# The order of transfers on SyncE in a two-layer graph network: the graph result first, an output's reads one slot later

## The reference: what is computed

```
x = layernorm(x + (adj @ x) @ W0 + b0)
h = x
for _ in range(3):
    a = adj @ h                            # a_in and a_out are the same here
    av = concat([a, a])
    z  = sigmoid(av @ w3.T + w3_b + h @ u3.T + u3_b)
    r  = sigmoid(av @ w4.T + w4_b + h @ u3.T + u3_b)
    hv = tanh(av @ w5.T + w5_b + (r * h) @ u5.T + u5_b)
    h  = (1 - z) * h + z * hv
out = layernorm(x + h)
```

## Time and profile before

| | |
|---|---|
| device time, median of 3 runs | 1645.3 us (1638.58, 1645.3, 1648.38) |
| the profiled execution: its own time | 1646.79 us |
| its span, first to last instruction | 1645.0 us |
| granted TensorE clock, mean | 0.99 |
| busy: PE, DVE, ACT, POOL | 1603.0, 1425.3, 945.5, 262.0 us |
| the DMA queue's packets | 50.4% of 16 engines' span |

### The profile page before, as it was taken

The page is one execution under the profiler, slowest core; times in us unless marked ns, Lnnn a source line. Parts: engine busy times, 40 slices in busy tenths (PEclk is TensorE's granted clock), DMA queues, the critical chain, the costliest instruction groups (busy, mean ns, idle before and its releaser), DMA issues.

```text
span 1645.0 us, 21680 instructions
## 1 busy us (share of the span) xinstructions
PE 1603.0 (97%) x7676; PEld 1350.1 (82%) x7676; DVE 1425.3 (87%) x1902; ACT 945.5 (57%) x1365; POOL 262.0 (16%) x296
## 2 busy tenths in 40 slices
PE   8899999999999999999999999999999999999994
PEld 8788888888888888888888888888888888888883
DVE  5788889898898898888989889899889898898886
ACT  3665555555565666555655556565556555655553
POOL 4011111122111121111211111112021121110002
PEclk9999999999999999999999999999999999999997
DMA  5343536555355653565535564455644555445543
GB/s 165 103 149 133 167 103 197 175 183 174 112 185 192 195 173 111 162 209 187 179 109 173 184 202 152 140 168 177 207 151 144 179 181 178 128 161 172 180 166 115
DMA packets 195132, 268.26 MB, mean 163 GB/s; under 512 B 18896, under 2 KB 166864, under 8 KB 195024
## 3 DMA queue, kind: packets, MB, share of 16 engines
q1 hardware_dynamic: 195024, 266.88, 50.4%
HBM read 134.68 MB, written 132.12 MB: 162 GB/s over the span
## 4 chain that ended last, share of the span: by engine, by line
PE 78%; DMA 10%; DVE 6%; SPq 4%; issue 1%; ACT 1%; POOL 0%; ACTq 0%; DVEq 0%; POOLq 0%
PE ps_r L316 38%; PE ps_h L316 25%; PE ps_a L376 6%; PE ps_l L342 5%; SPq L219 3%; PE ps_l L331 2%; DMA h_scratch_a<-h_blocks_a 2%; DMA h_scratch_b<-h_blocks_b 2%; DMA h_scratch<-h_blocks 2%; DMA a_landed<-a_scratch_a 2%; DVE a_blocks L696 1%; DMA a_landed<-a_scratch_b 1%; DVE hv L736 1%; DVE hv L733 1%; DMA x_in_b<-x 1%
## 5 line engine op out<-in xcount | busy, mean ns | idle before, releaser
L563 ACT ACTIVATE rh<-ps_r,bias_r 128x512 f32<-128x512 f32 x192 | 132.3, 690 | 131.0 <-PE ps_r L316 130.9
L473 ACT ACTIVATE rh_hi<-rh 128x512 fp32r<-128x512 f32 x192 | 119.1, 634 | 121.0 <-DVE rh L724 120.8
L696 DVE STREAM_TRANSPOSE a_blocks<-ps_a 128x512 f32<-128x512 f32 x184 | 119.9, 690 | 70.9 <-PE ps_a L376 70.9
L579 ACT ACTIVATE hv<-ps_h,bias_h 128x512 f32<-128x512 f32 x192 | 129.1, 688 | 50.9 <-PE ps_h L316 50.6
L840 POOL TENSOR_TENSOR out_var_eps_sb<-out_meanvar,eps 128x4 f32<-128x4 f32 x32 | 6.4, 201 | 832.4 <-DVE out_meanvar L649 832.4
L638 DVE TENSOR_TENSOR rh_lo<-rh,rh_hi 128x512 fp32r<-128x512 f32 x192 | 125.7, 690 | 9.5
L736 DVE TENSOR_TENSOR hv<-hv,z_sb 128x1024 f32<-128x1024 f32 x96 | 117.7, 1226 | 10.4 <-DVE hv L733 0.5
L316 PE MATMUL ps_r<-h_hi,u_hi 128*128 128x512 f32 x384 | 119.6, 393 | 7.3 <-ACT z_sb L575 7.3
L316 PE MATMUL ps_r<-a_hi_a,w_hi 128*128 128x512 f32 x384 | 120.7, 396 | 5.7 <-ACT rh L563 5.7
L575 ACT ACTIVATE z_sb<-ps_r,bias_z 128x512 f32<-128x512 f32 x192 | 120.6, 676 | 5.5 <-PE ps_r L316 5.5
L316 PE MATMUL ps_r<-a_hi_b,w_hi 128*128 128x512 f32 x384 | 119.7, 393 | 0.0
(11 more groups left out here) (271 smaller groups left out, 4006.5 us busy)
## 6 DMA issues: line engine op xcount, KB each, us to landing
h_scratch_a<-h_blocks_a SPq DMA_DIRECT2D x48, 512.0 KB, 4.6
h_landed_a<-h_scratch_a SPq DMA_DIRECT2D x192, 128.0 KB, 2.9
h_scratch_b<-h_blocks_b SPq DMA_DIRECT2D x48, 512.0 KB, 3.6
h_landed_b<-h_scratch_b SPq DMA_DIRECT2D x192, 128.0 KB, 2.8
a_scratch_a<-a_blocks SPq DMA_DIRECT2D x46, 512.0 KB, 2.7
a_landed<-a_scratch_a SPq DMA_DIRECT2D x184, 128.0 KB, 3.0
a_scratch_b<-a_blocks SPq DMA_DIRECT2D x46, 512.0 KB, 2.6
a_landed<-a_scratch_b SPq DMA_DIRECT2D x184, 128.0 KB, 2.8
```

The source lines that it names most:

```text
L473: return act.activation(dst, src, ACT.Copy)
L563: act.activation(rh[:, c, :], ps_r[:, c, :], ACT.Sigmoid, bias=bias_r[:, c:c + 1]).then_inc(r_ready, 1)
L579: act.activation(hv[:, c, :], ps_h[:, c, :], ACT.Tanh, bias=bias_h[:, c:c + 1]).then_inc(hv_ready, 1)
L696: tr = dve.transpose(a_blocks[:, :, c, :].rearrange("p i (b e) -> p i b e", e=Q), ps_a[:, c, :].rearrange("p (i b f) -> p i b f", b=G, f=Q))
```

## The change

The loop of SP is written in another order, and `move_h` is cut in two, `write_h` and `read_h`. In each slot the write of `a` now comes ahead of the write of `h0`, and the reads of `a` ahead of those of `h0`. A state after steps 1 and 2 is moved as before. An output's write stays at the end of its slot, but its reads go to the next slot, behind that slot's two writes and ahead of the reads of `a`. No transfer is added, taken away or changed in size, and no other engine's list changes.

```diff
-            def move_h(m):
+            def write_h(m):
                 half = m % 2
                 sp.wait_ge(h_blocks_ready, m + 1)
                 if m >= 2:
                     sp.wait_ge(h_moved[half], (m // 2) * MOVED)
                 to_dram(h_scratch[half], h_blocks[half][:, :, :], h_written[half])
+
+            def read_h(m):
+                half = m % 2
                 sp.wait_ge(h_written[half], (m // 2 + 1) * 16)
...
             for s in range(END + 1):
                 h0_next = group_at(s, NORM + 1) if s + 1 >= FOUR else s + 1
-                if h0_next is not None:
-                    write_h0(h0_next)
+
                 if FOUR <= s + 1 < SLOTS:
                     write_a(s + 1)
                 if h0_next is not None:
-                    read_h0(h0_next)
+                    write_h0(h0_next)
+                for g in output_at(s, 1):
+                    read_h(nth_move[g, STEPS - 1])
                 if FOUR <= s + 1 < SLOTS:
                     read_a(s + 1)
+                if h0_next is not None:
+                    read_h0(h0_next)
                 for g in output_at(s, STORE):
                     store(g)
                 if (g := group_at(s, GRAPH - 2)) is not None and g > FOUR:
                     load(g)
                 if 1 <= s <= SLOTS and at(s - 1)[1] < STEPS - 1:
-                    move_h(nth_move[at(s - 1)])
+                    write_h(nth_move[at(s - 1)])
+                    read_h(nth_move[at(s - 1)])
                 for g in output_at(s, 0):
-                    move_h(nth_move[g, STEPS - 1])
+                    write_h(nth_move[g, STEPS - 1])
```

## The result

The changed kernel takes 1633.4 us (median of 6 runs, 1632.7 to 1635.1) against 1645.8 for the kernel before in the same comparison. One of the six executions of before took 3298.4 us; without it the median is 1645.3, and the ratio is taken without it. The ratio is 0.993, with a 95% interval of 0.991 to 0.995: 0.7% faster. I had forecast 1640.0 with a range of 1637 to 1651, and had given 0.80 to a difference too small to tell from none. The direction holds; the gain was 11.9 us where I had forecast 5.3, and the range missed it.

What follows compares the result with a forecast made beforehand. PE was taken as the bound, busy 1603.0 of 1645.0 us, with only 7.3 us of waits for z to win. 1645.0 - 7.3 + 0.5 = 1638.2 of span, plus 1.8 around it, gave 1640.0 us; range 1637 to 1651.

Steps and rivals of the forecast that it cites:

- The term -7.3: PE's seven listed waits for z, at places 4 and 7, would all go, saving 7.3 us.
- The threshold: Latest landing of `a` that costs PE no wait for z: about +11.3 us from the end of the slot's transposes.
- the 0.5 us left in for late transfers: Allowance of 0.5 us added to the forecast for late single transfers such as slot 55's.
- Parts 1 to 3: SP's reordered writes and reads in heavy slots: `a` lands at about +9.9 us, so all seven waits for z go.
- rival A: Full DMA queue not in order: `a` shares engines with h0's reads, lands up to 2.7 us later; about 1672 us, chance 0.06.
- Its half: Half of rival A's delay: `a` at +11.9 in 26 slots, 0.6 us each, giving 1655 us; no chance of its own.
- Rival B: Full queue slower than its parts: `a` 2 us later, at +11.9, in 7 of 28 slots; 1643.5 us, chance 0.18.
- The 1.8 us of later landing: HBM access of 2 us at high load, not 0.2, could land `a` up to 1.8 us later in a fuller queue.
- Step 4: DVE's next `a_blocks` ends at +16.5, 1.5 us behind PE's pace, covered by the following slots at no cost.
- Step 5: State moved at places 1, 4, 7 lands later, delaying the next `a`; fits by 0.9 us, priced at 0.
- rival C: State's reads hold the next slot's `a`; PE waits 1 us at places 2, 5, 8; 1660 us, chance 0.06.
- Step 6: At the end, slot 94, `a` lands 1.2 us later behind the output's reads; cost 0 us, at most 0.6.

Runs made afterwards that it cites:

- z late: Against the changed kernel, no transfer moved; ACT makes four copies into a spare buffer between `a_hi` and z in 28 heavy slots: 1665.6 us, ratio to before 1.011.

## Why the prediction was right and wrong

**What bounds the kernel: right in mechanism, wrong in size.** The prediction's sentence was that "a change of SP's order can win at most 7.3 us, 0.4%, unless it shortens the ends". This step failed. The term -7.3 was read off the list of waits, and it measured 9.9 in the middles of the same two profiles. By the starts of the matmuls the seven waits cost 9.2 us, 0.3 each more than the list has, and the short delays in slots 89 and 92, on no list of z, 0.6. The miss is 2.6 us.

The threshold has the same fault: PE was 2.0 us late in slot 55, not 1.74, so the latest landing that costs nothing is +11.0, not +11.3. With a's reads last, slots 46 and 52 took `a` at +11.6, landed at +11.5, and PE lost 0.5 us in each. Nor does it hold "for 28 slots alike": in slots 88 and 91 some 0.3 us were lost at +10, through DVE. The latest landing of the changed kernel, +10.9 in slot 82 of its second profile, left 0.1 us to the true threshold: that not one slot paid was in part luck.

**The profile as a stand-in for the median: wrong.** I wrote that the rest of the idle time is start and tail and subtracted from 1645.0. But 3.3 us of that start came from 6.8 us at half clock, which the program has in some executions. It hid that this profile had the fewest waits of three: the middles of before were 1498.5, 1506.3 and 1504.5. In the two other profiles before pays 16 to 18 us for its waits and what follows them, rather than the 9.9 of the first. For the profiled execution the account closes: 2.6 + 3.3, and the 0.5 us left in for late transfers, which the changed kernel never needed, are 6.4, and 1640.0 - 6.4 = 1633.6. I held the spread of the runs of before (1638.6 to 1648.4) for the waits' and used it only to say that it goes away; it should have told me that one profile was one draw.

**Parts 1 to 3, the landing of a: right.** Forecast +9.9; landed in the median at +9.4, in slot 55 at +10.4, at the latest at +10.9, and no wait for z in 28 heavy slots in two profiles. The order of service in the queue and the prices of 1.37 and 2.7 us held, and the run with `a`'s reads last held them to it. So rival A, shared engines, is out: it needed an average of +11.3. Its half has an error of sum: half of 2.7 gives +11.25, inside the prediction's own threshold, not +11.9. Rival B is out with it: at places 4 and 7 `a` landed at +9.1 to +10.5 in the first profile, so at most 0.6 of the 2 us was left. The 1.8 us of later landing that the prediction weighed beside them (9.9 + 1.8 is +11.7, not +11.6) did not come as a whole in any slot.

**Step 4, DVE 1.5 us behind: right.** 2.1 behind in slot 56, 0.6 to 1.1 in slots 11, 14, 17 and 20, and on PE's pace by slot 58.

**Step 5, the state's later move, and rival C: right for this kernel, by a margin that is real.** I forecast the state's landing at +19.6 and the next write of `a` 2.1 us behind PE's pace; measured +19.9, and 2.6 behind, as the state's write went out at +8.9 and not at +7.2. `a` of slot 56 landed at +25.3 (forecast +25.2), and the transposes behind it ended on PE's pace, at +32.8. PE did not wait, though at place 5 `a` was once taken at +10.5. The run with `a` first moved the state's landing 4.3 us further (slot 73) and lost 10.5 us of the middle by it and by the late `a` behind it. Rival C was the right danger with the wrong kernel.

**Step 6, the end: right.** 0.1 us.

**The range.** It was bounded below by the floor that I had computed, less 3 us. A floor computed from one list is itself an estimate, and the range should have had the start and the waits' true price as unknowns of their own.

## What to carry to other kernels

In a queue that serves in order, each reader has a latest landing that costs nothing; work out that time for all readers, and again for each stretch with a pace of its own, before moving one transfer ahead, since giving one more than it needs takes it from the next. Fill the wait between a write and its own reads with other transfers, rather than putting both first. Price a stall by the distance between instruction starts, not by the list of waits, and compare two profiles of the same kernel before taking one as its median.

## What the runs showed of the hardware that was not expected

- After an idle time of 1.8 to 3.0 us in the middle of the program, PE ran at half clock for some 3.4 us in some cases: after listed waits of 2.5 us (second profile of before), 2.96 and 1.89 us (third), 2.07 and 2.89 us (a's reads last) and 1.80 us (z late), with a granted clock of 0.50 to 0.51 in windows behind them. Each costs about 1.7 us on top of the wait. The length of the wait alone does not decide it: waits of 2.21 us (a's reads last) and 2.03 us (z late) had a granted clock of 1.00 behind them.
- The same program, before, had 0, 3.4 or 6.8 us at half clock in its first 20 us, and opened slot 3 accordingly at 92.0, 93.9 or 96.0.
- SP's issue of a read group takes 1.73 us in most places, but 2.9 to 3.0 us in nearly every slot of the changed kernel in which it stands right behind two writes (2.96 in slot 55, 2.95 in slot 73). What causes it is not shown: the run with only a ahead of h0 has one of 3.10 us, at 1517.18, with no write open in front of it.
